# Mamba mixer on one core: the 16 dt columns move into a unit of z, which is run third in a block, and the softplus moves forward with them

## The reference

```python
z, xBC, dt = split(u @ W_in.T)            # 1024, 1024 + 2*128, 16 columns; u is the layernorm of x
xBC = silu(causal_conv4(xBC) + conv_b)    # 10 chunks of 128 channels: B, C and 8 of x
dt_s = softplus(dt + dt_bias)             # one value per token and head
dA = exp(dt_s * A)
state = dA * state + x * (dt_s * B)       # scan over tokens, 16 heads of 64
y = (C . state + x * D) * silu(z)
out = rmsnorm(y) * norm_w @ W_out.T
```

## Time and profile before

| | |
|---|---|
| median of 3 runs | 1470.63 us (1470.34 to 1471.83) |
| the profiled execution, its own time | 1477.63 us |
| span of its trace | 1475.6 us |
| projection part of the second block, 622.22 to 678.02 us of the trace | 55.80 us, PE busy 55.74 |

### The profile page before, as it was taken

The page is one execution under the profiler, slowest core; times in us unless marked ns, Lnnn a source line. Parts: engine busy times, 40 slices in busy tenths (PEclk is TensorE's granted clock), DMA queues, the critical chain, the costliest instruction groups (busy, mean ns, idle before and its releaser), DMA issues. The chain is left out here.

```text
span 1475.6 us, 23088 instructions
## 1 busy us (share of the span) xinstructions
PE 1413.8 (96%) x8754; PEld 1220.8 (83%) x8754; DVE 976.0 (66%) x1680; ACT 780.0 (53%) x1289; POOL 826.3 (56%) x496
## 2 busy tenths in 40 slices
PE   6999999999999899999999999889999999999998
PEld 5877999998987777788778779669879999998887
DVE  6484445445557898889879879966755444455466
ACT  3313666666632366575756656744115666666511
POOL 3202888887735544834753663662016887877543
PEclk9899999999999999999999999999999999999999
DMA  8232777777754220021012011006135877777444
GB/s 322 86 121 88 254 291 284 266 267 277 260 164 114 86 83 19 16 72 44 1 58 72 2 44 58 10 32 243 38 124 185 300 258 284 296 274 276 143 133 171
DMA packets 66782, 225.74 MB, mean 153 GB/s; under 512 B 7536, under 2 KB 15728, under 8 KB 65264
## 3 DMA queue, kind: packets, MB, share of 16 engines
q1 hardware_dynamic: 44592, 166.58, 31.4%
q0 software_dynamic: 11360, 37.23, 8.2%
q10 hardware_dynamic: 10720, 20.45, 3.7%
HBM read 187.01 MB, written 37.22 MB: 152 GB/s over the span
## 5 line engine op out<-in xcount | busy, mean ns | idle before, releaser
L651 POOL TENSOR_TENSOR g_lo<-g_raw,g_hi 128x1408 fp32r<-128x1408 f32 x54 | 187.8, 3478 | 95.3 <-ACT g_hi L819 92.7
L651 POOL TENSOR_TENSOR u_lo<-u_raw,u_hi 128x1408 fp32r<-128x1408 f32 x54 | 174.5, 3231 | 40.1 <-ACT u_hi L819 40.1
L681 POOL DMA_INDIRECT xg<-token_x,row_of x78 | 110.2, 1413 | 140.4 <-DVE row_of L1299 123.6
L1849 PE MATMUL bank<-u_hi,xgT 128*128 128x352 f32 x624 | 168.4, 333 | 0.0
L1849 PE MATMUL bank<-g_hi,xgT 128*128 128x352 f32 x624 | 162.7, 323 | 0.0
L1872 PE MATMUL bank<-d_hi,hT 128*128 128x512 f32 (+1 forms) x468 | 158.3, 392 | 4.7 <-DVE hT L1154 4.7
L1154 DVE TENSOR_TENSOR hT<-bank,hT 128x384 fp32r<-128x384 f32 x78 | 43.5, 557 | 165.8 <-ACT hT L819 165.8
L1154 DVE TENSOR_TENSOR d_lo<-d_raw,d_hi 128x1536 fp32r<-128x1536 f32 x54 | 130.3, 2413 | 21.1 <-ACT d_hi L819 13.3
L864 ACT ACTIVATE gate<-bank 128x512 f32<-128x512 f32 (+1 forms) x48 | 28.7, 597 | 216.7 <-PE bank L1802 199.1
L737 POOL TENSOR_TENSOR w_hl<-w_raw,w_hl 128x1024 fp32r<-128x1024 f32 x35 | 89.8, 2567 | 90.3 <-ACT w_hl L819 90.3
L1817 PE MATMUL bank<-d_hi,hT 128*128 128x512 f32 x352 | 116.7, 401 | 4.6 <-DVE xs L1154 2.2
(11 more groups left out here) (262 smaller groups left out, 3475.0 us busy)
## 6 DMA issues: line engine op xcount, KB each, us to landing
d_raw<-in_w_down SPq DMA_DIRECT2D x54, 768.0 KB, 5.8
g_raw<-in_w_gate SPq DMA_DIRECT2D x54, 704.0 KB, 6.6
u_raw<-in_w_up SPq DMA_DIRECT2D x54, 704.0 KB, 6.8
w_raw<-in_w_in SPq DMA_DIRECT2D x36, 512.0 KB, 3.7
routed_y<-ys ACTq DMA_DIRECT2D x32, 512.0 KB
token_x<-xn SPq DMA_DIRECT2D x8, 1024.0 KB, 5.7
X<-in_x SPq DMA_DIRECT2D x4, 1024.0 KB, 10.4
turned_x<-tmpT SPq DMA_DIRECT2D x16, 256.0 KB, 4.1
```

Of the source, the lines that this page charges most:

```text
L651: pool.tensor_tensor(half_of(piece, 1, s), raw_at[piece][s % RING][:], half_of(piece, 0, s).bitcast(F), ALU.subtract)\
L681: pool.indirect_dma_start(xg[:, n % XG], None, token_x, bass.IndirectOffsetOnAxis(ap=row_of[:, at:at + 1], axis=0))\
L1849: ins = pe.matmul(dst[:, 0:FE], xgT[:, n % 2, hx, kc], half_of(piece, hw, NS + j)[:, kc], start=(m == 0), stop=(m == 3 * KD - 1))
```

## The change

The separate product for dt is gone. Its 16 columns of `W_in` are appended to unit 5, the first of z, which then has 272 columns (`WD`), and dt comes out with the tokens on the partitions, with no transpose. The 272 columns of a token tile don't fit twice in one bank, so the four token tiles of this unit go to banks 6, 7, 4 and 5. The unit moves from step 5 to step 3. The first part of the softplus moves behind the 4th convolution, the exponential to the 5th (`c == 4` in ACT's loop), and the polynomial behind the 6th. `w_raw` and `w_hl` are 272 columns wide in every unit, of which 256 are loaded, split and used in the others; `pre` moves into the space of `L`. The diff, cut; first the constants and the load:

```diff
+WD = WU + HEADS
+DT_UNIT = 5
+DT_BANKS = (6, 7, 4, 5)
-ORDER = (0, 1, 2, 3, 5, 4, 6, 7, 8)
+ORDER = (0, 1, 5, 2, 3, 4, 6, 7, 8)
...
-                    sp.dma_start(w_raw[:, w % 2], w_in[ORDER[w % NWU]]).then_inc(m_raw[w % 2], 16)
+                    wide = width(ORDER[w % NWU])
+                    sp.dma_start(w_raw[:, w % 2, :, 0:wide], w_in[ORDER[w % NWU], :, :, 0:wide]).then_inc(m_raw[w % 2], 16)
```

ACT, `z_out`:

```diff
+                        if u == DT_UNIT:
+                            for q in (2 * half, 2 * half + 1):
+                                ins = act.activation(zs[:, q, 0:WU], bank[DT_BANKS[q]][:, 0:WU], ACT.Silu)
+                            ins.then_inc(m_z, 1)
+                            return
```

ACT, the loop over the steps and convolutions:

```diff
-                                    if (u, c) == (3, 7):
+                                    if (u, c) == (1, 3):
                                         unit_hi(w + 2)
...
                                     if 1 <= c < NCH - 1:
                                         conv_out(n - 1, c - 1)
+                                    if c == 4:
+                                        after(m_dx, j + 1, BPB)
+                                        act.activation(d_e[:], d_z[:], ACT.Exp).then_inc(m_de, 1)
...
-                                if u == 1:
-                                    after(m_dtT, j + 1, BPB)
-                                    after(m_yd, max(j * TB - 1, 0), TPB - 1)
-                                    act.activation(dtT, bank[3][0:HEADS, :], ACT.Copy).then_inc(m_dtc, 1)
```

DVE, `softplus` and the loop over the convolutions:

```diff
-                            after(m_dtp, j + 1, BPB)
-                            own.step(dve.tensor_tensor(three(d_x), bank[2][:, 0:NQ].rearrange("p (q h) -> p q h", h=HEADS),
-                                                       some(hp[:, 0:HEADS], TB), ALU.add))
+                            after(m_z, j * 8 + 2, 8 * BPB)
+                            for q in range(TB):
+                                own.mark(dve.tensor_tensor(d_x[:, q * HEADS:(q + 1) * HEADS], bank[DT_BANKS[q]][:, WU:WD],
+                                                           hp[:, 0:HEADS], ALU.add))
+                            own.join()
...
-                            if c == NCH - 5:
+                            if c == 3:
                                 softplus()
-                            if c == NCH - 3:
+                            if c == 5:
                                 log1p()
```

TensorE, the loop over the steps:

```diff
-                                if u == 1:
-
-                                    pe.wait_ge(m_wdt_lo, 1)
-                                    for m, (kc, (hw, hx)) in enumerate([(c, h) for c in range(KD) for h in HALVES]):
-                                        ins = pe.matmul(bank[3][0:HEADS, :], wdt[:, hw, kc], xb[:, hx, kc],
-                                                        start=(m == 0), stop=(m == 3 * KD - 1))
-                                    ins.then_inc(m_dtT, 1)
-                                if u == 2:
-                                    after(m_dtc, j + 1, BPB)
-                                    after(m_res, j * TB, TPB)
-                                    for q in range(TB):
-                                        ins = pe.matmul(bank[2][:, q * HEADS:(q + 1) * HEADS], dtT[:, q * P:(q + 1) * P],
-                                                        ident[0:HEADS, 0:HEADS], start=True, stop=True)
-                                    ins.then_inc(m_dtp, 1)
...
                                         for kc in range(KD):
                                             for hx, hw in HALVES:
-                                                ins = pe.matmul(bank[place][:, (q % 2) * WU:(q % 2 + 1) * WU],
-                                                                xb[:, hx, kc, q * P:(q + 1) * P], wt[:, hw, kc],
+                                                ins = pe.matmul(dst, xb[:, hx, kc, q * P:(q + 1) * P],
+                                                                wt[:, hw, kc, 0:width(u)],
```

More of the change, by code:

```diff
@@ L275, in program @@
     xD = mx("xD", [P, DI])
-    dtT = xD[0:HEADS, 0:D]
     ysq = mx("ysq", [P, DI], B16)
@@ L285, in program @@
     wd = mx("wd", [P, NQ])
-    w_raw = mx("w_raw", [P, 2, KD, WU])
+    w_raw = mx("w_raw", [P, 2, KD, WD])
     S = mx("S", [P, 2, DI])
@@ L304, in program @@
     mx_x = placer(xs1_at)
-    w_hl = mx_x("w_hl", [P, 2, 2, KD, WU], R)
-    pre = mx_x("pre", [P, 2, TAPS - 1 + D])
+    w_hl = mx_x("w_hl", [P, 2, 2, KD, WD], R)
+    pre = nc.alloc_sbuf_tensor_at("pre", [P, 2, TAPS - 1 + D], F, offset=L[:].tensor.manual_sbuf_range[0])
     place_of = lambda t: t[:].tensor.manual_sbuf_range
@@ L498, in turn_waits, with width @@
         return after
+    def width(u):
+        return WD if u == DT_UNIT else WU
     block = nc.Block()
@@ L974, in mixer @@
                 act.wait_ge(m_raw[0], 16)
-                split_hi(w_hl[:, 0, 0], w_raw[:, 0], m_whi)
+                split_hi(w_hl[:, 0, 0, :, 0:WU], w_raw[:, 0, :, 0:WU], m_whi)
                 for piece in range(4):
@@ L988, in unit_hi @@
                             after(m_zp, jj * 8 + (u - 5) * 2 + 2, 8 * BPB)
-                        split_hi(w_hl[:, w % 2, 0], w_raw[:, w % 2], m_whi)
+                        cols = slice(0, width(ORDER[w % NWU]))
+                        split_hi(w_hl[:, w % 2, 0, :, cols], w_raw[:, w % 2, :, cols], m_whi)
                     def conv_in(n, c):
@@ L994, in conv_in @@
                         after(m_cp, n + 1, BPB * NCH)
+                        if c == 0:
+                            after(m_E, 2 * (n // NCH) * TB, 2 * TPB)
                         after(m_conv, n - 1, BPB * NCH)
@@ L2106, in turn @@
                                         after(m_sums, j + 1, BPB)
-                                    if u == 5:
+                                    if u == DT_UNIT and half == 0:
                                         wait_residual(pe, k)
```

54 lines of the change are left out of this document (24 added, 30 removed).

## The result

| | before | with the change |
|---|---|---|
| median | 1471.23 us of 4 runs (1470.34 to 1472.18) | 1494.98 us of 4 runs (1490.25 to 1500.60) |
| ratio | 1 | 1.0154, 95% interval 1.0127 to 1.0180 |
| profiled execution, own time / span | 1477.63 / 1475.6 us | 1495.04 / 1493.0 us |
| mean granted clock in it | 0.987 | 0.981 |

The kernel is 23.75 us slower by the medians, 1.6%; the ratio is that of the means, and counts the traced execution of before among its runs. The two traced executions differ by 17.4 us only, since the traced one of before is 6.4 above its median. So places are read from the traces, and sizes from the medians, except where the text says that a size is a trace's.

The account below looks back on a forecast made before the run. TensorE was taken to set the length; the four stretches, +5.3 twice, +4.4 and +3.6, sum to 18.6 us, less 2.6 coming back: 16.0 slower, 1470.63 + 16.0 = 1486.6 us, range 1476 to 1497.

Parts of the forecast that it names:

- the wait that I named: Ahead of step 7 TensorE waits 6.1 us for weights held behind the Silu of the 7th convolution in ACT's list.
- TensorE sets the length: In the four projection parts, a microsecond taken from TensorE is one won, as long as nobody makes it wait.
- The walk: Second block timed step by step from its start at 622.22: end at +61.1 against 55.80 before, +5.3 us.
- two low halves in the polynomial: POOL low halves holding DVE during the polynomial: one assumed; two, as before, would make it +25 us.
- What comes back behind them: Behind each projection part, the last Silu comes less late after the spread: 0.65 us a block, 2.6 in all.
- the first rival's break-even: In TensorE's list, weights of step 7 landing at +43.45 would make the change neither gain nor lose.
- The polynomial's place: DVE's 10.02 us polynomial stood before at the one place where ACT doesn't need what comes behind it.
- TensorE as the bound: In the projection parts TensorE stays the bound and 10.3 us are saved: 1460.3 us, chance 0.09.
- the cancelling of waits and saving: Across the blocks, unseen overlap gives 4 to 5 us each: 1468 to 1473 us, chance 0.04.
- The drain: Ahead of ACT's exponential, a table switch costs 1.37 us more a block: 1492.1 us, chance 0.05.
- The late loads: Weight loads with short 1 KB rows take up to 8.2 us and come late: near 1518 us, chance 0.08.
- The saved 3.45 us: On TensorE per block, dt product and transposes removed, less 0.32 for added columns; 13.8 us in all before waits.

Follow-up runs that it names:

- kernel 3: The changed kernel with 22 unused matmuls of 512 columns between steps 6 and 7, where TensorE waits: 1487.64 us, 1.0103.
- kernel 1: The changed kernel with the polynomial back behind the 8th convolution: 1496.68 us, 1.0157.
- kernel 9: Halo copies moved from DVE to ACT, made twice: in the version with z and dt at step 4, 1473.57 us; in the kernel before, 1467.85 us.
- kernel 7: The kernel before with z moved from step 5 to step 3, dt product and transposes kept, exponential behind the 6th convolution's Silu: 1485.77 us, 1.0090.
- kernel 8: The changed kernel with the polynomial behind the 8th convolution and 18 unused matmuls ahead of the decay sums: 1485.92 us, 1.0094.
- kernel 4: The changed kernel with the z unit that carries dt at step 4, softplus behind the 6th convolution, polynomial behind the 8th: 1479.50 us, 1.0041.
- kernel 2: The changed kernel with the high half of step 7's weights ahead of the Silu of the 7th convolution in ACT's list: 1496.00 us, 1.0163.
- kernel 5: The changed kernel with the order of before, dt in z at step 5, softplus and exponential behind the 8th convolution, polynomial behind the 9th: 1502.04 us, 1.0192.
- kernel 6: The version with z and dt at step 4, with the exponential moved behind the high half of step 7's weights: 1487.43 us, 1.0088.

## Why the prediction was right, and where it was not

The prediction was 1486.6 us, 16.0 slower, with a range of 1476 to 1497. The median is 1494.98, 23.75 slower than 1471.23: the direction was right, and so was the wait that I named; the size was short by a third, and the sentence from which I started, that TensorE sets the length, was wrong.

- **The walk** held to within 0.7 us at each point of the second block up to step 7. Foreseen and read: step 4 +24.1 and +24.1; the polynomial's start +34.25 and +34.0, its end +42.1 and +41.6; step 7 +48.75 and +48.2; the wait ahead of step 7 6.1 and 5.44, ahead of step 6 2 and 1.59. One low half held DVE in the polynomial (2.13 us), as I took it, and not two or none.
- **The missing term is the clock.** I gave step 7 the 5.97 us of the earlier trace rows, a row at full clock, and looked nowhere at what TensorE does after 6 us without work. It took 7.2 us more over four blocks in the trace; kernel 3, where the wait is filled, is 7.3 us faster and lies at 1487.64, 1.0 from my number (against its own runs of before it is 14.0 slower, where I had 16.0). No row of before showed step 7 after a long wait, but its windows had a clock column, and I used only the rows in which it read 1.00.
- **Luck in the range.** 1494.98 lies inside my range because its upper end allowed for two low halves in the polynomial. The trace shows one; what filled that room was the clock, which I had not counted.
- **The rest of the sum.** In the traces the parts are 22.4 us longer, 15.2 without the clock's 7.2, against my 18.6; part of that is the weights of step 7, which came 0.5 us sooner a block. What comes back behind them is 0.66, 1.44 and 0.71, against my 0.65 a block. The traces' sum is thus 19.6 us (412.26 and 431.85 in the table), and the medians say 23.75. The 4 us between lie outside this stretch. They are less than the 7.9 us by which the rest of the span differs among the twelve traces, and the runs of before that were made beside the experiments have medians 2.3 to 3.0 us above the 1471.23 taken here; no run tells more of it.
- **The step that failed** is the first, "TensorE sets the length, and a microsecond taken from it is one won", and with it the first rival's break-even, +43.45 for the weights of step 7. In kernel 1 they were there at +43.40, and the kernel was 1.6% slower. I had seen that DVE is "nearly a second bound", 0.57 us behind, and then costed only TensorE's wait for weights. The decay sums' wait for DVE's `aparts` was not in the walk at all, and it was there before the change. Two rows of the kernel before, first and third block:

```profile
553.02 0.51 PE L2012 MATMUL bank<-tri_b,aparts 128*96 128x128 bf16 x6 [0.77 <-DVE aparts L1541]
...
793.49 0.51 PE L2012 MATMUL bank<-tri_b,aparts 128*96 128x128 bf16 x6 [0.41 <-DVE aparts L1541]
```

In all four blocks of before the sums start 0.15 us after DVE's last cast ends, the same distance as in kernel 1's first block, where TensorE visibly waits for it. Up to the sums step 7 takes 6.78, 5.97, 6.32 and 5.97 us there, and 5.75 in each block once DVE is relieved (kernel 9). So DVE's polynomial already set the end, and the slack was none, not 0.57. Kernels 1, 7 and 8 show that DVE's chain (the data of the 5th convolution, the convolutions, the polynomial) sets the end in this order too, and kernel 7 that the order costs 4.1 us in the second block, with the dt product still in place.

- **The polynomial's place**, which I told the reader to keep in mind, decides which step waits. Kernel 1 put it back where ACT needs nothing of what follows, and won nothing.
- **The rivals.** TensorE as the bound falls (waits of 23.9 us). So does the cancelling of waits and saving. The drain falls: 1.30 us from the load's start to the exponential, which follows with no gap; the 2.66 us of the Trainium skill, page "ScalarE: Activation LUTs", section "What ACT_TABLE_LOAD costs", are not what this trace shows. The late loads fall: 3.8 us in the median, 3.7 before.
- **The saved 3.45 us** a block were worth nothing in kernel 1, and less than nothing by comparison with 7 (1496.68 and 1485.77 us, 430.89 and 423.56 in the table). In kernel 4, where z stands in the middle, the waits are short and the saving about covers them.

So of the 19.6 us in the traces 11.3 come from the order alone (kernel 7 less before), and 8.3 are what happens when TensorE's work is taken out of a chain that another engine sets. Kernel 3 gives 7.4 of these back, and kernel 8 gives 7.8 back to kernel 1, each by filling the wait. The medians say 11.5 for the order (1485.77 less 1474.24), and 7.3 and 10.8 for the two fillings.

What stays open: the 4 us between the traces and the medians, and what decides whether the clock falls after a wait of about 2 us. That the clock is what makes the runs of one kernel differ was not tested.

## What to carry to other kernels

Before an engine's work is taken away, look for the chain that ends just behind it (here DVE's rows, 0.57 us ahead of TensorE, and its polynomial, for which TensorE already waited 0.2 to 1.0 us a block). A busy share of 55.74 in 55.80 us doesn't rule such a chain out. With no slack the saving is worth nothing, and the engine to relieve is the other one, as the halo copies show. A data source that is moved up pushes others back, so follow every consumer of what is pushed to the end of the part; a wait that vanishes at one place has to be looked for at the next before a gain is booked. And a wait of TensorE is to be costed with the time that the step behind it takes at the lower clock.

## What was not expected of the hardware

- After waits of 5.4 to 5.5 us the 48 matmuls of step 7 in the changed kernel took 7.3 to 8.5 us, where they take 5.8 with the wait filled (kernel 3): 1.5 to 2.7 us a time, a quarter to a half of the wait. In kernels 1, 2, 5 and 6 the 48 matmuls of step 8, behind the sums and waits of 4.5 to 5.6 us, took 6.7 to 8.1. The granted clock was 0.50 in the first 2.2 us of the step (the changed kernel) and 0.51 in the first 3.35 (kernel 1).
- After waits of 1.8 to 2.3 us the clock fell in some blocks and not in others (step 7 of kernels 7 and 9).
- 18 or 22 matmuls per block without any use made a kernel 10.8 and 7.3 us faster.
- The mean clock and the time of a run go together in one and the same kernel: of 12 runs of the kernel before with the copies on ACT, four with a clock of 0.994 took 1459.8 to 1461.6 us, and one with 0.987 took 1470.88.
